# Two single batches and three pairs in the expert groups; ScalarE counts whole turns; the sums in one 1,024-wide addition; bulk loads behind the first blocks

## The reference

```python
x = x + 0.5 * ffn(layernorm(x))
x = x + attention(layernorm(x))
x = x + 0.5 * ffn(layernorm(x))
```

```python
logits = xf @ gate_w
top_logits, top_idx = jax.lax.top_k(logits, K)
top_gates = jax.nn.softmax(top_logits, axis=-1)
h = gelu(jnp.einsum('nd,edh->neh', xf, w1) + b1)
out_e = jnp.einsum('neh,ehd->ned', h, w2) + b2
routed = jnp.einsum('ne,ned->nd', gates, out_e)
shared = gelu(xf @ shared_w1 + shared_b1) @ shared_w2 + shared_b2
```

```python
phi = k_val[..., None] * theta
re_k, im_k = (jnp.cos(phi), jnp.sin(phi))
merged = jnp.concatenate([p_w.squeeze(-1), (pw5 * re_k).reshape(b, l, FLAT), (pw5 * im_k).reshape(b, l, FLAT)], axis=-1)
cs = jnp.cumsum(merged, axis=1)
out_re = jnp.sum(state_re * q_re + state_im * q_im, axis=-1)
out_im = jnp.sum(state_im * q_re - state_re * q_im, axis=-1)
```

## Time and profile before

| | |
|---|---|
| Median of 3 runs | 1228.48 us (1225.8 to 1231.84) |
| Profiled execution, its own time | 1230.61 us |
| Its span (first to last instruction) | 1229.1 us |
| Mean granted TensorE clock | 0.939 of full speed |
| Busy: PE, DVE, ACT, POOL | 84%, 59%, 54%, 39% |

### The profile page before, as it was taken

How to read it: one execution, slowest core, us unless ns; L and a number is a source line. 1 busy time by engine, 2 the same in 40 slices (tenths; PEclk the granted TensorE clock), 3 DMA queues, 4 the chain that set the end, 5 groups by cost and what they waited for, 6 DMA issues and landing times. The chain is left out here.

```text
span 1229.1 us, 11345 instructions
## 1 busy us (share of the span) xinstructions
PE 1027.5 (84%) x3424; PEld 563.1 (46%) x3424; DVE 727.2 (59%) x1206; ACT 658.5 (54%) x1112; POOL 485.3 (39%) x452
## 2 busy tenths in 40 slices
PE   4939999858999679799878979987978898679993
PEld 2526545534445445344534534444555543336661
DVE  3500016699799699689969977897979920300000
ACT  2414325578556487454866774446579851314441
POOL 4335431353533443250733312634364420165552
PEclk9969999988999889989979989899989999789997
DMA  8886571666744666843765827256686663125666
GB/s 274 320 283 113 98 163 50 170 150 119 159 126 117 181 154 109 210 115 101 202 155 106 208 77 171 53 169 139 137 188 148 101 121 70 58 64 109 112 111 103
DMA packets 68976, 172.53 MB, mean 140 GB/s; under 512 B 12354, under 2 KB 12354, under 8 KB 66790
## 3 DMA queue, kind: packets, MB, share of 16 engines
q0 software_dynamic: 32576, 72.44, 32.6%
q1 hardware_dynamic: 36342, 99.38, 26.7%
HBM read 112.86 MB, written 68.33 MB: 147 GB/s over the span
## 5 line engine op out<-in xcount | busy, mean ns | idle before, releaser
L859 PE MATMUL yps<-w_all,hidden_sb 128*128 x424 | 210.7, 621 | 43.6 <-ACT hidden_sb L1025 43.5
L843 PE MATMUL hps<-w_all,hidden_sb 128*128 x848 | 209.3, 391 | 22.5 <-ACT hidden_sb L1025 18.4
L1612 POOL DMA_INDIRECT xs<-x_normal,rows_i x106 | 131.7, 1242 | 210.4 <-PE xps L834 159.5
L843 PEld LDWEIGHTS hps<-w_all,hidden_sb 128*128 128x128 f32 x848 | 161.2, 195 | 76.5 <-issue 58.7
L1414 DVE TENSOR_TENSOR_SCAN run<-pwx,trig 128x512 f32<-128x512 f32 x128 | 149.2, 1206 | 12.8 <-ACT trig L1111 12.5
L1636 POOL DMA_INDIRECT x_rows<-ys,rows_i x56 | 100.1, 1788 | 119.3 <-ACT ys L1038 110.3
L859 PEld LDWEIGHTS yps<-w_all,hidden_sb 128*128 128x128 f32 x424 | 79.5, 197 | 120.5 <-issue 117.9
L1038 ACT ACTIVATE ys<-yps,slots 128x512 f32<-128x512 f32 x106 | 72.8, 689 | 96.2 <-PE yps L859 86.6
L801 PE MATMUL yps<-sw_sb,hidden_sb 128*128 128x512 f32 x256 | 123.9, 628 | 0.0
L789 PE MATMUL hps<-xnT,sw_sb 128*128 128x512 f32 x256 | 118.2, 610 | 0.7 <-ACT hidden_sb L998 0.7
L834 PE MATMUL xps<-ident,xs 128*128 128x128 f32 x424 | 66.5, 281 | 41.1 <-DMA xs<-x_normal,rows_i 33.5
(11 more groups left out here) (200 smaller groups left out, 1597.3 us busy)
## 6 DMA issues: line engine op xcount, KB each, us to landing
qx<-q_cols SPq DMA_DIRECT2D x128, 256.0 KB
x_normal<-xin SPq DMA_DIRECT2D x32, 256.0 KB, 4.1
w_all<-in_w_experts SPq DMA_DIRECT2D x8, 1024.0 KB, 7.3
xin<-x_rows SPq DMA_DIRECT2D x32, 256.0 KB, 7.1
turns_sb<-in_w_out SPq DMA_DIRECT2D x3, 1536.0 KB, 12.7
xin<-in_x SPq DMA_DIRECT2D x16, 256.0 KB, 4.6
sum_rows<-ys SPq DMA_DIRECT2D x16, 256.0 KB, 4.1
xin<-sum_rows POOLq DMA_DIRECT2D x16, 256.0 KB, 9.0
```

The costliest lines, as they stand in the source:

```text
L843: t = PE.matmul(hps[:, bank, 0:H], xT[:, j % 2, c, :], w_all[:, bass.ds(expert[j] + c * H, H)], start=c == 0, stop=c == KC - 1)
L859: t = PE.matmul(yps[:, bank, :], hb[:, j % 2, ec, :], w_all[:, bass.ds(expert[j] + (KC * H + ec * D), D)], start=ec == 0, stop=ec == EC - 1)
L1612: GE.indirect_dma_start(xs[:, j % NX, :], None, xn_rows[PAIR_OF[g]], bass.IndirectOffsetOnAxis(rows_i[:, g % 2, j:j + 1], 0)).then_inc(*xs ...
```

## The change

1. **Groups.** Jobs 2 and 3, before in groups of their own, form one group; there are then 15+15+23+23+23 = 99 blocks where there were 15x4+23x2 = 106. The fetch of job 3 comes ahead of `a_load` of batch 1, and the attention of batch 2 waits for the blocks of both jobs.
2. **Whole turns.** The multiplication by theta that is stored as int32, on VectorE until now (line 1401), becomes a Copy with a scale on ScalarE (`count_turns`, stage `c_int`). VectorE keeps the fused multiply and subtract.
3. **Sums.** The real sum is written beside the imaginary one in `qx`, and both are added to `outT` in one instruction, 1,024 wide, where there were two of 512. The difference (imaginary) now comes first, the real sum waits for it, since it writes over one of its inputs, and the wide addition waits for the real sum.
4. **Opening.** GpSimd's tables come in two parts, the ones that routing needs first. The experts' weights stand right behind the first loads in SP's queue; the weights of the gate matrices (`w_bd`) and the rows of batches 1 to 3 that stand ready for `add` (`w_rows`) wait for the third block of group 0. A group's scatters (8 for a single job, 16 for a pair) are cut into parts of 4, and group 1's stand behind the first blocks' gathers.
5. **Order.** Pieces at the head of the attention get 2,000 more on their way, and some costs are changed.

```diff
-    GROUPS = [[0], [1], [2], [3], [4, 5], [6, 7]]
+    GROUPS = [[0], [1], [2, 3], [4, 5], [6, 7]]
...
-        TURNS = [("fetch", 0), ("fetch", 1), ("a_load", 0), ("fetch", 2), ("a_load", 1), ("fetch", 3),
+        TURNS = [("fetch", 0), ("fetch", 1), ("a_load", 0), ("fetch", 2), ("fetch", 3), ("a_load", 1),
...
-            piece("POOL", ("w_rest",), 9.0, ("POOL", ("load", 0)))
+            piece("POOL", ("w_tables",), 3.0, ("POOL", ("load", 0)))
+            piece("POOL", ("w_rest",), 6.0, ("POOL", ("w_tables",)))
             piece("SP", ("w_rest",), 3.6, ("POOL", ("w_rest",)))
             for e in range(E):
-                piece("SP", ("w_expert", e), 0.6, *([("SP", ("w_expert", e - 1), 4.0)] if e else [("SP", ("w_rest",))]))
-            piece("SP", ("w_bd",), 0.5, ("SP", ("w_expert", E - 1)))
-            piece("DVE", ("w_soft", 0), 1.0, ("POOL", ("w_rest",)))
+                piece("SP", ("w_expert", e), 0.6, ("SP", ("w_expert", e - 1) if e else ("w_first",), 4.4))
+            piece("SP", ("w_bd",), 0.5, ("PE", ("one", 0, 2)))
+            piece("DVE", ("w_soft", 0), 1.0, ("POOL", ("w_rest",)), ("DVE", ("rows", 0)))
             piece("ACT", ("w_soft", 0), 0.2, ("DVE", ("w_soft", 0)), table="exp")
             piece("DVE", ("w_soft", 1), 4.0, ("ACT", ("w_soft", 0)))
             for b in range(B):
-                piece("SP", ("w_rows", b), 0.5, ("SP", ("w_expert", E - 1) if b else ("w_bias",)))
+                piece("SP", ("w_rows", b), 0.5, ("PE", ("one", 0, 2)) if b >= len(GROUPS[0]) else ("SP", ("w_expert", E - 1)))
...
-            piece("POOL", ("scatter", g), 2.5 * GTS[g], ("DVE", ("place", g)), *[("DVE", ("gates", q)) for q in GROUPS[g]],
-                  ("SP", ("w_rest",), 3.0))
-            piece("SP", ("slots", g), 0.5, ("POOL", ("scatter", g), 3.0),
+            piece("DVE", ("place", g), 5.0 if NB < 16 else 6.5, ("PE", ("place", g)), *([("DVE", ("rows", 0))] if g == 1 else []),
+                  *([("PE", ("two", g - 2, NBS[g - 2] - 1)), ("POOL", ("scatter", g - 2, GTS[g - 2] // 2 - 1), 2.0)] if g > 1 else []))
+            for i in range(GTS[g] // 2):
+                piece("POOL", ("scatter", g, i), 5.1, ("DVE", ("place", g)), *([("POOL", ("bring", 0, 2))] if g == 1 else []),
+                      *[("DVE", ("gates", q)) for q in GROUPS[g]], ("SP", ("w_rest",), 3.0))
+            piece("SP", ("slots", g), 0.5, ("POOL", ("scatter", g, GTS[g] // 2 - 1), 3.0),
...
-            piece("DVE", ("c_turn", b, n), 1.3, ("DVE", ("a_mem", b, half)), *free, *([] if i else [("DVE", ("w_soft", 1))]))
+            piece("ACT", ("c_int", b, n), 0.7, ("DVE", ("a_mem", b, half)), *free, *([] if i else [("DVE", ("w_soft", 1))]))
+            piece("DVE", ("c_turn", b, n), 0.8, ("ACT", ("c_int", b, n)))
...
+                if k[1][0] in ("a_load", "a_stats", "a_norm", "a_turn", "a_mem", "a_p", "a_fall", "a_q", "a_spread"):
+                    way[k] += 2000.0
...
+            def count_turns(b, n):
+
+                half, m = divmod(n, M)
+                if b > 0 or n >= 2:
+                    last = STEPS_OF[STEPS_OF.index((b, n)) - 2]
+                    act.wait_ge(*added.at((*last, 0)))
+                act.wait_ge(*convolved.at((b, half, CW - 1)))
+                if (b, n) == (0, 0):
+                    act.wait_ge(*weighing.at(21))
+                SE.activation(trig_int[:, n % 2, 0, :], kept(b, half), ACT.Copy,
+                              scale=theta_sb[:, half, m:m + 1]).then_inc(*turns_counted.of((b, n)))
...
-                if b > 0 or n >= 2:
-                    last = (b, n - 2) if n >= 2 else (b - 1, STEPS + n - 2)
-                    vec.wait_ge(*(out_summed if last[1] % M else added).at((*last, 0)))
-                vec.wait_ge(*convolved.at((b, half, CW - 1)))
-                VE.tensor_scalar(trig_int[:, s, 0, :], kept(b, half), th, None, ALU.mult).then_inc(*phase_int.of((b, n)))
-                vec.wait_ge(*phase_int.at((b, n)))
+                vec.wait_ge(*turns_counted.at((b, n)))
...
                 re2, im2 = trig[:, n % 2, :, :], qx[:, n % NQX, :, :]
-                re = outT[:, half, 0, :] if m == 0 else re2[:, 0, :]
-                im = outT[:, half, 1, :] if m == 0 else im2[:, 0, :]
+                re, im = [outT[:, half, i, :] if m == 0 else im2[:, i, :] for i in range(2)]
                 if m == 0 and b > 0:
                     vec.wait_ge(*y_made.at((b - 1, half * VH + VH - 1)))
-                vec.wait_ge(*real_made.at((b, n)))
-                VE.tensor_tensor(re, re2[:, 0, :], re2[:, 1, :], ALU.add).then_inc(*added.of((b, n, 0)))
                 vec.wait_ge(*imag_made.at((b, n)))
                 VE.tensor_tensor(im, im2[:, 0, :], im2[:, 1, :], ALU.subtract).then_inc(*added.of((b, n, 1)))
+                vec.wait_ge(*real_made.at((b, n)))
+                vec.wait_ge(*added.at((b, n, 1)))
+                VE.tensor_tensor(re, re2[:, 0, :], re2[:, 1, :], ALU.add).then_inc(*added.of((b, n, 0)))
 
             def sum_parts(b, n):
                 half = n // M
-                re, im = outT[:, half, 0, :], outT[:, half, 1, :]
                 vec.wait_ge(*added.at((b, n, 0)))
-                VE.tensor_tensor(re, re, trig[:, n % 2, 0, :], ALU.add).then_inc(*out_summed.of((b, n, 0)))
-                vec.wait_ge(*added.at((b, n, 1)))
-                VE.tensor_tensor(im, im, qx[:, n % NQX, 0, :], ALU.add).then_inc(*out_summed.of((b, n, 1)))
+                VE.tensor_tensor(outT[:, half, :, :], outT[:, half, :, :], qx[:, n % NQX, :, :],
+                                 ALU.add).then_inc(*out_summed.of((b, n)))
...
+                for i in range(4 * part, 4 * part + 4):
+                    r, t = divmod(i, GTS[g])
+                    GE.indirect_dma_start(
+                        slots_dram[g], bass.IndirectOffsetOnAxis(dest_i[:, g % 2, t, r:r + 1], 0),
+                        told[:, g % 2, first_tile + t, r, :], None).then_inc(*scattered[g % 2].of((g, t, r)))
...
                 elif stage == "w_bd":
+
+                    sp.wait_ge(*one_made.at((0, 2)))
                     SP.dma_start(wbd_sb[:, :, :, :], w_bd).then_inc(*bd_loaded.of(0))
...
+                    if at[0] >= len(GROUPS[0]):
+                        sp.wait_ge(*one_made.at((0, 2)))
```

107 lines of the change are left out of this document (52 added, 55 removed).

## The result

The changed kernel takes 1247.49 us (median of 4, 1242.55 to 1249.82) where the one before took 1229.57 in the same session: a ratio of 1.0144, 95% interval 1.0101 to 1.0186, so slower by 1.4%. I had forecast 1215 and a range that ended at 1238. The profiled execution has a span of 1244.8, 15.7 more than before.

A forecast was written before the change was run, and what follows sets the result against it. PE with the blocks was taken to bound up to batch 2's statistics, with VectorE waiting, and PE and its waits to set the end. Terms +2 −11 −5 = −14 took the span from 1229.1 to 1215.1, forecast 1215; range 1194 to 1238.

The forecast's parts named there:

- The opening: Start to group 0's end: first block at about 61 instead of 81.6 (−20), group 0 ending 10 us earlier.
- rival 1: Opening keeps its gain: gathers don't suffer from the bulk, group 0 ends at 131.7, time 1205; chance 0.15.
- Rival 2: Sums on VectorE: wide addition pays in full, dependence costs nothing, a step saves 0.65 us, time 1201; chance 0.06.
- rival 5: Second half, batch 2's first scan to last output scaled: gains up to 20 us, time 1199 to 1205; chance 0.09.
- To the end of the pair group: Group 0's end to batch 2's first scan: statistics at 557, first scan at 619 for 616.8, +2 us.
- the term for the waits: Group 0's end to the pair's last block: 19 us of PE waits go, fuller ScalarE adds 7.
- rival 3: Pair group ends later: waits stay, statistics of batch 2 begin 12 to 13 us later, time 1228; chance 0.15.
- the wait from the last block to the statistics: Pair's last block on PE to batch 2's statistics on VectorE: 24 us, as in the kernel before.
- the stretch behind: Batch 2's statistics to its first scan: 103.7 us shrinks by 44 to 60, as steps and job 3's work come earlier.
- So I cost it at nothing there.: Second half: the conversion's added ScalarE time, net +12 us over the span, is covered by other work.
- Rival 4: Conversion comes late in ScalarE's queue, holding VectorE 0.8 to 1 us a step: 1238 to 1247; chance 0.13.
- Tail: Last output scaled to the end: product some 5 to 7 us earlier, job 6's second product fills idle; −5 us.

The follow-up runs named there:

- b_opening_same: Kernel before with only the later part of the opening (group 1's scatters behind the sixth gather, bulk behind the third block), same orders otherwise: ratio 0.9951.
- a_load4_late: Changed kernel with one VectorE stage, job 4's row statistics, moved behind the first scan and products of batch 2: ratio 1.012 to the kernel before.
- b_hop_012: Kernel before, same work, planned anew with the planner's allowance for a semaphore at 0.12 us in place of 0.1: ratio 1.0167.
- b_hop_008: Kernel before, same work, planned anew with the planner's allowance for a semaphore at 0.08 us in place of 0.1: ratio 1.0274.
- b_conv_act: Kernel before with only the conversion to whole turns moved to ScalarE, planned anew: ratio 1.0119.
- a_old_groups: Changed kernel with the old groups (106 blocks) and old TURNS, planned anew: 1274.85 us, ratio 1.0327 to the kernel before.
- b_pair: Kernel before with only jobs 2 and 3 in one group and the new TURNS, planned anew: 1265.62 us, ratio 1.0272.
- b_pair_2000: Kernel before with jobs 2 and 3 in one group, the new TURNS and the 2,000 for the attention's head, planned anew: 1273.56 us, ratio 1.0335.
- a_old_step: Changed kernel with conversion and sums as before, planned anew: 1264.07 us, ratio 1.0233 to the kernel before.
- a_hop_012: Changed kernel, planned anew with the planner's allowance for a semaphore at 0.12 us in place of 0.1: 1229.58 us, ratio 0.9977 to the kernel before.
- a_conv_dve: Changed kernel with the conversion to whole turns back on VectorE, same orders: 1247.39 us, ratio 1.0113 to the kernel before.
- b_no_conv: Kernel before with the conversion left out altogether (phase zero, sums not the reference's), same orders: ratio 1.0091.

## Why the prediction was wrong

**What held.** The opening: first block at 59.55 (61 forecast), group 0's end 9.5 earlier (10). In the first number two errors cancel: the first gather came at 55.85 (54 forecast) and landed in 3.7 us, not 7. In the second the size was right and the cause was not mine. I had charged it to starting, draining and weights; the 12.5 us more inside group 0 (84.5 for 72.0) are 9.2 of idle time on PE (13.8 for 4.6) and 3.3 of work that took longer, at a clock of 0.90 for 0.97. The added idle time is one wait. The window in which the bulk went out, and ScalarE in it:

```profile
74.80:95.00 20.20, 12.56 (x54) 8.34 (x52) 0.00 (x0) 5.08 (x12) 12.24 (x12) 0.87 1.01 364
```

```profile
95.22 0.69 ACT L1045 ACTIVATE ys<-yps,slots 128x512 f32<-128x512 f32 x1 [10.87 <-DMA sum_rows<-ys,into_i]
```

The addition of a block to `sum_rows`, issued at 79.25, landed after 15.9 us, where such an addition takes 4.9 without the bulk; so its buffer `ys` came free late, ScalarE waited 10.87 us for it and PE 9.07 for ScalarE. The two gathers issued beside the bulk took 15.0 and 16.3 us for 4.3, but PE waited for neither. So rival 1 did not come: b_opening_same, with the same wait (10.34 us, for an addition to `x_rows`), lost 17.5 us inside the group where it had won 17 ahead of it. There the eight scatters of group 1 also held GpSimd from 71.7 to 81.6; what they cost was not separated. The rule that the Trainium skill states in "DMA: Bandwidth & Descriptors" ("Queues, rings and completion order"), that an engine serves its queues in turn, did not keep gathers and additions free of the bulk here, by these landing times; how the packets took turns, no run showed.

Rival 2 falls: on VectorE dependence costs, and more than I took. From the start of the first product to the next scan a step took 663.11−658.43 = 4.68 and takes 556.12−551.07 = 5.05, +0.37 where I had +0.28: the real sum began 0.10 behind the end of the difference and not 0.03. So a step saves 0.13 and not 0.22. The second half gained 17.3, within the bounds of rival 5; why, no run shows. The output product ended 50.9 behind the last scaling for 55.8, the 5 forecast.

**Where it failed: the step "To the end of the pair group".** I forecast the first scan of batch 2 at +2; it came 33 later. Three terms of the sum were off.

The first is the term for the waits, −19 with +7 for ScalarE. Up to the end of the pair PE's busy time rose by 350.28−287.43 = 62.9, near the 66 forecast. Its idle time was to fall by 12 and rose by 1.7 (50.0 for 48.4). So the 19 us did not go; they stood elsewhere. That is rival 3, and its statistics at 569.5 are near the 572.2 measured.

The second is the wait from the last block to the statistics: I took 24, it was 28. The DMA engines were at 1.01 of their time, but before at 1.00, so this is not the difference. On VectorE the statistics now stand behind an output scaling, which waited 9.50 us (570.87) until batch 0's output rows, now as late as the pair's end, had left `tail_sb`; the statistics followed without a further wait.

The third is the stretch behind, which was to shrink by 44 and shrank by 26. I had counted 3.6 steps of batch 1 in it; the trace of before has six scans there (533.24 to 604.82), and three of them are left in the changed kernel, since VectorE was 17.5 us late, not early, at batch 1's ninth step (513.9 for 496.4), its scans having waited for the sine (64.8 for 12.8 in all). The two errors nearly cancel: VectorE's busy time in the stretch fell by 94.92−58.12 = 36.8, where I had taken out 38. What failed is again the waits: I took out 6 us, and its idle time rose by 10.7 (19.5 for 8.8). The wait of 10.24 for job 4's rows is as large, but a_load4_late took it away and won nothing clear of the noise.

That PE has little to do here while batch 2's attention starts, since job 3's work had been moved ahead of it, is seen with the pair in each plan. From the last block ahead of the statistics to the first scan of batch 2:

| kernel | us | PE busy | PE idle |
|---|---|---|---|
| before | 127.4 | 112.5 | 14.9 |
| b_hop_012, b_hop_008 | 125.9, 129.8 | 110.1, 112.6 | 15.8, 17.2 |
| b_conv_act, a_old_groups | 135.4, 121.8 | 110.4, 92.5 | 25.0, 29.3 |
| with the pair: changed, b_pair | 105.5, 130.1 | 51.6, 76.0 | 53.9, 54.1 |
| with the pair: b_pair_2000, a_old_step, a_hop_012 | 77.0, 78.0, 73.5 | 41.5, 41.9, 41.1 | 35.5, 36.1, 32.4 |

Yet this idle time does not decide the result. What a kernel with the pair costs in the end is the plan's: +18, +29, +33, +41 us (the changed kernel, a_old_step, b_pair, b_pair_2000) or nothing (a_hop_012).

**"So I cost it at nothing there."** The conversion on ScalarE, 0.72 us and not 0.66, 46.0 us in all:

```profile
L1120 ACT ACTIVATE trig<-kval,small_sb 128x512 int32<-128x512 f32 x64 | 46.0, 720 | 37.4 <-DVE qx L1456 22.5 <-DVE outT L1456 11.6 <-DVE kval L1369 3.3
```

Added alone, in the old orders, it costs 21 us, though VectorE has 30 less to do. 54% busy is no cover: ScalarE stands in the loop of every step and of every block. Rival 4 was right in kind in those orders, with 1.24 us of waiting a step, but only 21/64 = 0.33 us a step of it reached the end. In the changed kernel's orders its sign did not come: `c_turn` waited 4.2 us in all, the scans did the waiting, and with the conversion back on VectorE (a_conv_dve) the time stayed. So the term was wrong for the old orders, by 21 us; in the changed kernel's it is not what made it slow.

**What the sum left out.** Every term was worked out for an edit in an order that stays. Here each edit runs the scheduler again. Without any edit that moves the old kernel by +20 or +33 us and the changed one by −20: more than my whole sum (−14) and more than the result (+18). With five plans in all, three of the old work (ratios 1, 1.0167, 1.0274) and two of the new (1.0144, 0.9977), the new work can't be called slower: shown is that this plan of it is slower than that plan of the old, and the plan alone is enough for the whole of the 1.4%. The range should have held it; it was made from the terms' bounds alone.

**Tail.** The 5 us won up to the last output rows were lost right behind them: job 7's transposes follow 20.3 us behind (1068.34−1048.0) where it was 15.6. GpSimd, ScalarE and PE of the changed kernel there:

```profile
1059.81 0.24 POOL L1602 TENSOR_SCALAR rstd_ffn<-rstd_ffn 128x4 f32<-128x4 f32 x1
```

```profile
1060.43 0.60 ACT L1061 ACTIVATE ys<-yps 128x512 f32<-128x512 f32 x1 [10.17 <-PE yps L808]
1060.93 2.92 ACT L1068 ACTIVATE xin<-xin,rstd_ffn 128x512 f32<-128x512 f32 x4
```

```profile
1060.76 3.70 PE L808 MATMUL yps<-sw_sb,hidden_sb 128*128 128x512 f32 x8
...
1064.81 3.70 PE L808 MATMUL yps<-sw_sb,hidden_sb 128*128 128x512 f32 x8
```

ScalarE's wait of 10.17 us stands ahead of job 7's rows (L1068), but it costs at most 0.9: GpSimd has the factors for these rows only at 1060.05. ScalarE begins them 12.9 us behind the last output rows, for 14.6 before. But PE, which was free at this place in the kernel before, now has two portions of job 6's second product ahead of the transposes, until 1068.5. That product, which stood between the output rows before, is what won the 5 there and lost them here; I had it fill idle time only.

**Open.** What it is in one order that makes it 20 or 33 us longer than another with the same work. Why b_no_conv takes longer with less work. Whether the clock is cause or result: in the 67 executions of the kernel before that go with the experiments, the time rose by 8.4 us for each 0.01 of clock lost (correlation −0.74), and the changed kernel's clock is some 0.016 lower; by that slope it would be 13 us, but a_hop_012 is 20 us faster than the changed kernel at a clock of 0.921, so the clock does not decide by itself.

## What to carry to other kernels

When an order comes out of a planner, plan the old work two or three times with a harmless number changed before weighing any edit: the spread is the smallest effect that an edit can be blamed for, and single waits in a trace (10 us taken away, nothing won) are a poor guide below it. To cost an edit itself, keep every engine's order and change one thing.

A batch of work moved ahead of a dependence is also taken away from behind it: ask what fills that place afterwards. A low busy share does not make an engine's time free when it stands in the loops between the others: 41 us of work added to ScalarE at 54% cost 17. And a large transfer moved out of the way of the first block is beside the later ones: look at what waits for a buffer there.

## What the runs showed of the hardware

The multiplication of 128x512 float32 to int32 takes 0.47 us on VectorE and 0.72 on ScalarE. A 1,024-wide addition that waits for the 512-wide one ahead begins 0.04 us behind its end (554.98 after 554.25+0.69). Beside a bulk load that kept the DMA engines at 1.01 of their time (74.8 to 95.0), two gathers of 128 rows landed in 15.0 and 16.3 us and an addition in 15.9, where they take 4.3 and 4.9. The 67 executions of the kernel before spread from 1224.3 to 1242.3 us, and about half of that spread goes with TensorE's mean granted clock (8.4 us for 0.01, correlation −0.74).
